# Scores of four heads at once on four row parts of the array, tanh and exp in place in a ring of eight

## What is computed

```
q = rms_norm(split_heads(x @ w_q.T));  k = rms_norm(split_heads(x @ w_k.T));  v = split_heads(x @ w_v.T)
scores = einsum('bhqd,bhkd->bhqk', q, k) / sqrt(8)
scores = tanh(scores / 50) * 50
probs  = softmax(where(causal, scores, -inf))
y      = einsum('bhqk,bhkd->bhqd', probs, v) ... @ w_o.T
x      = layernorm(x + y)
```

## Time and profile before

| what | value |
|---|---|
| runs of the kernel before | 831.39, 833.25, 834.76 us; median 833.25 |
| profiled execution, span from first to last instruction | 830.0 us (its own time is not listed beside the span; the median is 3.25 us above it) |
| PE busy | 678.9 us, 82% |
| DVE busy | 595.4 us, 72% |
| ACT busy | 554.2 us, 67% |
| POOL busy | 392.0 us, 47% |
| mean granted clock of TensorE | 0.828 of full speed |
| score matmuls (L1182) | 2,048, busy 193.1 us |
| tanh (L716) and exp (L731) | 256 and 128, busy 280.2 and 271.5 us |

### The profile page before, as it was taken

One profiled execution on the slowest core, in us unless ns is written; L12 is line 12 of the kernel. 1 busy time (PEld: TensorE's weight loads), 2 busy tenths in 40 slices (PEclk: granted clock), 3 DMA queues, 4 the chain that ended last, 5 costly groups with the idle time before them and its releaser, 6 DMA issues.

```text
span 830.0 us, 16995 instructions
## 1 busy us (share of the span) xinstructions
PE 678.9 (82%) x6576; PEld 401.4 (48%) x6576; DVE 595.4 (72%) x1681; ACT 554.2 (67%) x403; POOL 392.0 (47%) x399
## 2 busy tenths in 40 slices
PE   3588787889979988999899988998899879865652
PEld 2344334455546455645455545645565535434232
DVE  4442718777787788958888788769896986588455
ACT  0588688889768876959768876788687968600000
POOL 5263436447544574346455664446546543421201
PEclk8567678899789987989789987899799979985755
DMA  6321302033300503030304030120303030000001
GB/s 190 64 42 37 64 13 53 25 61 119 64 14 17 112 12 67 27 64 14 64 14 90 14 64 15 50 54 2 64 26 65 2 64 27 13 1 26 0 0 51
DMA packets 96913, 36.75 MB, mean 44 GB/s; under 512 B 68018, under 2 KB 94146, under 8 KB 96834
## 3 DMA queue, kind: packets, MB, share of 16 engines
q1 hardware_dynamic: 96834, 35.67, 18.8%
HBM read 14.69 MB, written 4.19 MB: 23 GB/s over the span
## 4 chain that ended last, share of the span: by engine, by line
PE 61%; DVE 18%; issue 10%; ACT 7%; POOL 3%; DMA 1%; POOLq 0%; DVEq 0%; ACTq 0%
PE ps_y L1199 16%; PE ps_s L1182 14%; ACT pr L731 4%; PE ps_m L1308 3%; PE ps_m L1230 3%; ACT th L716 3%; PE ps_m L1206 3%; PE ps_a L1230 3%; PE ps_m L1356 2%; PE ps_a L1393 2%; DVE v_aug L844 2%; PE ps_m L1258 2%; PE ps_a L1206 2%; PE ps_a L1258 1%; PE ps_a L1292 1%
## 5 line engine op out<-in xcount | busy, mean ns | idle before, releaser
L716 ACT ACTIVATE th<-ps_s 128x1024 f32<-128x1024 f32 (+1 forms) x256 | 280.2, 1129 | 110.7 <-PE ps_s L1182 102.0
L627 POOL TENSOR_TENSOR pr<-pr,tri 128x320 f32<-128x320 f32 (+1 forms) x256 | 194.8, 784 | 186.7 <-ACT pr L731 186.7
L731 ACT ACTIVATE pr<-th 128x2304 f32<-128x2304 f32 x128 | 271.5, 2122 | 15.5 <-PE ps_y L1199 15.4
L1182 PE MATMUL ps_s<-q_st,k_st 32*64 32x512 f16 (+7 forms) x2048 | 193.1, 319 | 24.9 <-ACT th L716 20.8
L1199 PE MATMUL ps_y<-pr,v_aug 128*32 128x512 f32 (+7 forms) x2048 | 157.4, 439 | 0.4 <-POOL pr L627 0.4
L1182 PEld LDWEIGHTS ps_s<-q_st,k_st 32*64 32x64 f16 x2048 | 92.3, 114 | 120.0 <-issue 54.3
L1199 PEld LDWEIGHTS ps_y<-pr,v_aug 128*32 128x32 f32 x2048 | 57.0, 113 | 66.9 <-issue 47.4
L641 POOL TENSOR_TENSOR st<-qk,st 128x1024 f16<-128x1024 f32 x32 | 73.8, 2327 | 32.3 <-DVE st L860 32.3
L629 POOL TENSOR_TENSOR k_wide<-qkT,head_of 128x1024 f32<-128x1024 f32 x16 | 30.1, 1902 | 58.0 <-DVE qkT L1029 58.0
L629 POOL TENSOR_TENSOR r<-x,rw_row 128x512 f32<-128x512 f32 x16 | 18.9, 1180 | 63.6 <-DVE x L922 63.6
L702 ACT ACTIVATE hq<-hu 128x512 f32<-128x512 f32 x8 | 5.0, 630 | 60.7 <-POOL hu L629 60.7
(11 more groups left out here) (220 smaller groups left out, 1133.9 us busy)
## 6 DMA issues: line engine op xcount, KB each, us to landing
x_in<-in_L_attn_x SPq DMA_DIRECT2D x16, 256.0 KB, 2.8
x_res<-in_L_attn_x SPq DMA_DIRECT2D x16, 256.0 KB, 3.1
result<-y_out SPq DMA_DIRECT2D x16, 256.0 KB, 2.4
mask_a<-in_L_ffn_attention_mask SPq DMA_DIRECT2D x3, 1024.0 KB, 5.2
pr<-in_L_ffn_attention_mask SPq DMA_DIRECT2D x2, 1024.0 KB, 8.6
w_sb<-in_L_ffn_w SPq DMA_DIRECT2D x2, 256.0 KB
q_st<-st SPq DMA_TRANSPOSE x16, 4.5
k_st<-st SPq DMA_TRANSPOSE x16, 4.7
```

What stands on the lines that cost most here:

```text
L627: return nc.gpsimd.tensor_tensor(buf, buf, tri[:, None, :].to_broadcast([P, blocks, 64]), ALU.mult)
L716: nc.scalar.activation(th[:, gi % 2, c0:c1], ps_s[:, c0:c1], ACT.Tanh, scale=1.0 / (QK_SCALE ** 2 * DH ** 0.5 * SOFTCAP))\
L731: nc.scalar.activation(pr[:, probs_at(n):probs_at(n) + GROUP], th[:, gi % 2, :], ACT.Exp, scale=SOFTCAP).then_inc(exp_done, 1)
L1182: last = mm(ps_s[64 * s:64 * s + 64, COL[kb]:COL[kb] + S - 64 * kb], k_st[rows, k, gi // 2, 64 * kb:64 * kb + 64], q_st[rows, k, gi // 2, ...
```

## The change

Two groups, an even one and the odd one behind it, now share four units (`UNIT_PRODUCTS`). In each unit the products of the even group (`one` = 0, row parts 0 and 1) alternate with those of the odd group (`one` = 1, row parts 2 and 3), and the two groups write separate banks of `ps_s`. Unit 0 is block 0 of both (banks 0 and 1). Unit 1 is blocks 1 and 7 of both (banks 2 and 4) and block 4 of the even group into bank 3. Unit 2 is blocks 2 and 6 of both. Unit 3 is blocks 3 and 5 of both and block 4 of the odd group. `th` is gone: tanh writes both groups' slots of `pr` at once, and exp works in place. The ring has eight slots all the time, the second mask has a buffer of its own, and a scratch area is set smaller, which makes room. An even group's first tanh waits for PV of the slots it is about to overwrite; no tanh waits for an exp any more. The masks of odd groups are four and two by two blocks. The core of the diff:

```diff
-COL = {0: 0, 1: 512, 7: 960, 2: 1024, 6: 1408, 3: 1536, 5: 1856, 4: 2048}
+COL = ({0: 0, 1: 512, 7: 960, 2: 1024, 6: 1408, 3: 1536, 5: 1856, 4: 2048},
+       {0: 0, 1: 512, 7: 960, 6: 1024, 2: 1152, 4: 1536, 5: 1792, 3: 1984})
 GROUP = 2304
-UNIT = ((0, 1024), (1024, GROUP))
-UNIT_BLOCKS = ((0, 1, 7), (2, 6, 3, 5, 4))
-SIX_FROM = 48
+RING = 8
+UNIT = ((0, 512), (512, 1024), (1024, 1536), (1536, GROUP))
+UNIT_BANKS = ((0, 1), (2, 4), (0, 1), (2, 4))
+UNIT_PRODUCTS = (
+    ((0, 0, 0), (1, 0, 512)),
+    ((0, 1, 1024), (1, 1, 2048), (0, 7, 1472), (1, 7, 2496), (0, 4, 1536)),
+    ((0, 2, 0), (1, 2, 640), (0, 6, 384), (1, 6, 512)),
+    ((0, 3, 1024), (1, 3, 2240), (0, 5, 1344), (1, 5, 2048), (1, 4, 1792)),
+)
...
-    return GROUP * (n % 5 if n < SIX_FROM else (5, 3, 4, 0, 1, 2)[(n - SIX_FROM) % 6])
+    return GROUP * (n % RING)
...
+        mask_b = sb("mask_b", [P, NT, S])
...
-        th = sb("th", [P, 2, GROUP])
-        pr = sb("pr", [P, 6 * GROUP + 256])
-        mask_b = pr[:, 5 * GROUP:5 * GROUP + NT * S].rearrange("p (c j) -> p c j", c=NT)
+        pr = sb("pr", [P, RING * GROUP + 320])
+        ring = pr[:, 0:RING * GROUP].rearrange("p (n c) -> p n c", c=GROUP)
...
+        def unit_banks(u):
+            if u < 3:
+                first, second = UNIT_BANKS[u]
+                return ps_bank[:, first:second + 1:second - first]
+            return ps_s[:, 2 * 512:5 * 512].rearrange("p (n c) -> p n c", n=2)
...
-                        causal(b.no * 8 + gi, 0, 512, 5)
-                        causal(b.no * 8 + gi, 960, 448, 3).then_inc(masked, 1)
+                        if gi % 2 == 0:
+                            causal(every(n, 0, 512, 5))
+                            causal(every(n, 960, 448, 3)).then_inc(masked, 1)
+                        else:
+                            causal(every(n, 0, 512, 4))
+                            causal(two_by_two(n, 960, 832, 192)).then_inc(masked, 1)
...
-                        for u, (c0, c1) in enumerate(UNIT):
-                            act.wait_ge(scores_ready, b.no * 16 + (2 * gi + u + 1))
-                            if gi >= 2 or b.at_least(1):
-                                act.wait_ge(exp_done, b.no * 8 + (gi - 1))
-                            nc.scalar.activation(th[:, gi % 2, c0:c1], ps_s[:, c0:c1], ACT.Tanh,
+                        n = b.no * 8 + gi - gi % 2
+                        if gi % 2 == 0 and n >= RING:
+                            act.wait_ge(pv_done, pv_of(n + 1 - RING))
+                        for half in range(2):
+                            u = 2 * (gi % 2) + half
+                            c0, c1 = UNIT[u]
+                            act.wait_ge(scores_ready, b.no * 16 + (2 * gi + half + 1))
+                            nc.scalar.activation(ring[:, n % RING:n % RING + 2, c0:c1], unit_banks(u), ACT.Tanh,
...
-                        act.wait_ge(tanh_done, b.no * 16 + (2 * gi + 2))
-                        n = b.no * 8 + gi
-                        if n >= 5 and n != SIX_FROM:
-                            act.wait_ge(pv_done, pv_of(n - (5 if n < SIX_FROM else 6)))
-                        if n == SIX_FROM:
-                            pe["sel"].wait(act, 1, "R")
-                        nc.scalar.activation(pr[:, probs_at(n):probs_at(n) + GROUP], th[:, gi % 2, :], ACT.Exp,
-                                             scale=SOFTCAP).then_inc(exp_done, 1)
+                        act.wait_ge(tanh_done, b.no * 16 + 4 * (gi // 2) + 4)
+                        probs = ring[:, (b.no * 8 + gi) % RING]
+                        nc.scalar.activation(probs, probs, ACT.Exp, scale=SOFTCAP).then_inc(exp_done, 1)
...
-                    t_.wait_ge(tanh_done, b.no * 16 + (2 * gi + u - 1))
-                for kb in UNIT_BLOCKS[u]:
+                    t_.wait_ge(tanh_done, b.no * 16 + (2 * gi + half - 1))
+                for one, kb, col in UNIT_PRODUCTS[2 * (gi % 2) + half]:
                     for s in range(2):
-                        rows = slice(32 * (2 * (gi % 2) + s), 32 * (2 * (gi % 2) + s) + 32)
-                        last = mm(ps_s[64 * s:64 * s + 64, COL[kb]:COL[kb] + S - 64 * kb],
+                        rows = slice(32 * (2 * one + s), 32 * (2 * one + s) + 32)
+                        last = mm(ps_s[64 * s:64 * s + 64, col:col + S - 64 * kb],
...
-    nc = _bacc.Bacc("TRN2", target_bir_lowering=False, num_devices=1)
+    nc = _bacc.Bacc("TRN2", target_bir_lowering=False, num_devices=1,
+                    dynamic_dma_scratch_size=4096)
```

More of the change, by code:

```diff
@@ L478, in at @@
             return {"a": ps_a, "m": ps_m}[BANK[use if unit is None else f"{use}/{unit.k}"]]
+        ps_bank = ps_s[:, :].rearrange("p (n c) -> p n c", c=512)
+        def unit_banks(u):
[3 more added lines that the diff above has]
+            return ps_s[:, 2 * 512:5 * 512].rearrange("p (n c) -> p n c", n=2)
         block = ctx.enter_context(nc.Block())
@@ L526, in _ @@
             load_mask(0, mask_a[:, :, :])
-            load_mask(1, mask_b)
+            load_mask(1, mask_b[:, :, :])
             def load_res(b, k):
@@ L571, in _ @@
                     if p == 1:
-                        load_mask(MASKS - 1, mask_b)
+                        load_mask(MASKS - 1, mask_b[:, :, :])
             for k in range(2):
@@ L621, in _, with causal, every, two_by_two @@
             pool.wait_ge(tri_ready, 4)
-            def causal(n, col, step, blocks):
-                buf = pr[:, probs_at(n) + col:probs_at(n) + col + step * blocks]\
-                    .rearrange("p (n c) -> p n c", c=step)[:, :, 0:64]
-                return nc.gpsimd.tensor_tensor(buf, buf, tri[:, None, :].to_broadcast([P, blocks, 64]), ALU.mult)
+            def causal(buf):
+                shape = list(buf.shape)
+                keep = tri[:, None, :] if len(shape) == 3 else tri[:, None, None, :]
+                return nc.gpsimd.tensor_tensor(buf, buf, keep.to_broadcast(shape), ALU.mult)
+            def every(n, col, step, blocks):
+                at_ = probs_at(n) + col
+                return pr[:, at_:at_ + step * blocks].rearrange("p (n c) -> p n c", c=step)[:, :, 0:64]
+            def two_by_two(n, col, far, near):
+                at_ = probs_at(n) + col
+                return pr[:, at_:at_ + 2 * far].rearrange("p (m c) -> p m c", c=far)[:, :, 0:2 * near]\
+                    .rearrange("p m (n c) -> p m n c", c=near)[:, :, :, 0:64]
             mul = lambda out, a, b: nc.gpsimd.tensor_tensor(out, a, b, ALU.mult)
@@ L682, in body @@
                         pool.wait_ge(exp_done, b.no * 8 + (gi + 1))
-                        causal(b.no * 8 + gi, 0, 512, 5)
-                        causal(b.no * 8 + gi, 960, 448, 3).then_inc(masked, 1)
+                        n = b.no * 8 + gi
+                        if gi % 2 == 0:
[4 more added lines that the diff above has]
+                            causal(two_by_two(n, 960, 832, 192)).then_inc(masked, 1)
                     for half in range(2):
@@ L1173, in setup_routed, with scores @@
                 mm(ps_y[:, 256:257], ones1[:, :], rb_one[:, :], start=True, stop=True).then_inc(setup_pe, 1)
-            def scores(b, k, gi, u):
+            def scores(b, k, gi, half):
                 if gi > 0 or b.at_least(1):
-                    t_.wait_ge(tanh_done, b.no * 16 + (2 * gi + u - 1))
-                for kb in UNIT_BLOCKS[u]:
+                    t_.wait_ge(tanh_done, b.no * 16 + (2 * gi + half - 1))
+                for one, kb, col in UNIT_PRODUCTS[2 * (gi % 2) + half]:
                     for s in range(2):
-                        rows = slice(32 * (2 * (gi % 2) + s), 32 * (2 * (gi % 2) + s) + 32)
-                        last = mm(ps_s[64 * s:64 * s + 64, COL[kb]:COL[kb] + S - 64 * kb],
+                        rows = slice(32 * (2 * one + s), 32 * (2 * one + s) + 32)
+                        last = mm(ps_s[64 * s:64 * s + 64, col:col + S - 64 * kb],
                                   k_st[rows, k, gi // 2, 64 * kb:64 * kb + 64], q_st[rows, k, gi // 2, 64 * kb:S],
@@ L1197, in pv @@
                         gi = 4 * half + j
-                        c = probs_at(b.no * 8 + gi) + COL[kb]
+                        c = probs_at(b.no * 8 + gi) + COL[gi % 2][kb]
                         last = mm(ps_y[32 * j:32 * j + 32, 64 * kb:S], v_aug[:, k, kb, gi, :], pr[:, c:c + S - 64 * kb],
```

## The result

Over four runs each the changed kernel took 808.3 us (807.7 to 809.85), the kernel before, on the same chip, 832.33 us (831.39 to 834.76): a ratio of 0.9715, with an interval of 0.9695 to 0.9735, or 24 us less. The forecast was 796, in a range of 772 to 831, with faster at 0.84.

A forecast was written before the change was run, and what follows sets the result against it. PE was taken to pace most of the scores, ACT much of the first two batch pairs. Scores 30 + ring 6 + ACT's order 1.4 = 37 us, from 830.0 to 793; with 3.25 for the median, 796 us, range 772 to 831.

The forecast's parts named there:

- Four products overlap: PE's scores: four heads run side by side on four row parts, units near 0.34 and 0.45 us.
- The rival of no overlap: PE's second couple of products queues behind the first; only ring and ACT order count, 7 us, 826 us; chance 7%.
- First-order gain: PE's score line: 37% off its 118.5 us of the chain of waits, 43.8 us.
- The share of it that arrives: Score saving reaching the end: 23 us after 201 us, 6 before, one after 701; 30 of 43.8 us.
- Ring: ACT's exp no longer waits for PV to free a ring slot: 6 us, out of 15.4 us of waits.
- ACT's order: ACT's tanh and exp: fewer waits on each other, a couple from 8.46 to 8.26 us; 1.4 us gained.
- No price for the clock: PE's granted clock: no term in the sum; a fall below 0.79 from 201 us was a slower rival, 8%.
- What would show it: Signs: shorter units, ACT's score waits well under 102.0 us, ACT above 82% busy, no exp PV waits, longer L1387 wait.
- No price for the masks: POOL's masks: eight blocks of 64 as before, 4+4 instead of 5+3 in odd groups, priced at nothing.
- DVE, ACT or lower clock eats most: Rival: PE gains but meets DVE's chains and ACT; 8 to 20 us left, 813 to 825 us; chance 15%.

The follow-up runs named there:

- four heads alone: Changed kernel's scores, masks and banks, but with the old ring and its waits and a third buffer of `th`: 810.13 us, ratio 0.974 to the kernel before.
- pairs of heads: Kernel before with only the ring changed (eight slots, tanh and exp in place), scores still in pairs of heads: 842.04 us, ratio 1.0112.
- filler: Products nobody reads, put on PE ahead of three waits for DVE; here added to the changed kernel with 64-column score products: 827.09 us, ratio 0.9933.

## Why the prediction was right, and where it was not

- **Four products overlap: right.** Units of 0.34 and 0.45 us were forecast and measured, and the four start within 10 ns. The rival of no overlap is out.
- **First-order gain: too small.** 43.8 us of score chain were to go; 64 went. The units at the high clock became shorter by the 35% forecast, and the line's part of the chain by 54%: some of its units are no longer on the chain, and other work ends last in their place.
- **The share of it that arrives: the step that failed.** "I keep three quarters of 84 x 0.37 = 31 us (23 us)" after 201 us. From the table, four heads alone give 6.9 us in the first two pairs (forecast: 6) and 16.7 us from there to the last score (forecast: 23 and 1). With the ring it is 14.2. The forecast took DVE's 86% as room in most places. But a busy share does not show a stretch such as the 3.29 us above, which shorter scores leave as it is: from 192 PE's busy time fell by 35 us (450.92 to 415.99), and its idle time grew by 21 (49.1 to 70.0). The doubt was put in words ("scores ahead of such a wait shrink into a longer wait") and priced too low. That the sum missed by no more is partly luck: 64 us left the chain where 43.8 were forecast, and 24 arrived where 37 were.
- **Ring, 6 us, and ACT's order, 1.4: mis-sized, together about 2.** ACT's couple is as forecast. Timeline of ACT (start us, us; x2 is two tanh):

```profile
409.79 1.92 ACT L750 ACTIVATE pr<-ps_s 128x1024 f32<-128x1024 f32 x2
411.60 2.12 ACT L760 ACTIVATE pr<-pr 128x2304 f32<-128x2304 f32 x1
413.62 2.36 ACT L750 ACTIVATE pr<-ps_s 128x1024 f32<-128x1024 f32 x2
416.01 2.12 ACT L760 ACTIVATE pr<-pr 128x2304 f32<-128x2304 f32 x1
418.04 1.92 ACT L750 ACTIVATE pr<-ps_s 128x1024 f32<-128x1024 f32 x2
```

From 409.79 to 418.04 us a couple takes 8.25 us, and 8.26 was worked out. No exp waits for PV. With the ring the first two pairs are 3.0 us shorter than with four heads alone, and the six behind them 2.5 us longer, so the gain is there and is lost again. With pairs of heads it is lost and more. That removing waits from ACT could make the kernel slower was no rival of the prediction.
- **No price for the clock: right in size.** 0.86 in the middle stretch against 0.88, worth some 6 us of PE's time at most, as worked out above.
- **What would show it:** units, their starts and PV waits came true, and the wait for `hn` grew, if only from 26.3 to 26.7 us; ACT's share, to be above 82%, is 81.7; ACT's wait for scores was to fall well under 102.0 us and is 103.7. That line measures whom ACT waits for, and PE, which stands idle 31 us more, still hands scores over late.
- **No price for the masks: held with four heads.** POOL's masks are 196.6 us in 256 instructions, 194.8 before. What was not seen is that their moment matters to DVE.

The 808.3 us lie inside the forecast's own 785 to 812, near its upper end. For the part that was lost, the rival "DVE, ACT or lower clock eats most" (8 to 20 us left) had the mechanism, as far as PE meets DVE's chains: 16 of the 31 us. Why PE's other waits grew was not tested.

## What to carry to other kernels

A line's share of the chain times its saving tells how much may leave the chain, not how much arrives: look at what the next engine does in its own order under that line, and count a shortened step at nothing wherever another engine's chain ends within the saving. To price the next bound, shorten that engine's work in the kernel before as well as in the changed one, and look whether the clock moved with it. A filler that is to raise the clock has a price of its own: count it. Measure the parts of a change alone and together; here one part was a loss by itself and about nothing beside the other.

## What was not expected of the hardware

DVE instructions of 0.29 us took 0.92 and 0.98 us when they began 0.02 and 0.03 us behind a mask of POOL. And less work on PE made the kernel slower: with score products of 64 columns the mean granted clock of the run went from 0.820 to 0.753 and the time from 808.3 to 824.5 us, and with the clock raised to 0.801 by filler, which takes 45 us of PE itself, the time stayed, at 827.1. Of 53 us of work that PE lost in the first of these, it is busy only 8 us less, for the lower clock.
